# Both halves of the product of states and receptance on VectorE, with new order tables

## The reference, cut to what matters

```python
def step(s, rkvw):
    r_t, k_t, v_t, w_t = rkvw
    a = k_t[:, :, :, None] * v_t[:, :, None, :]
    out = jnp.einsum('bhk,bhkd->bhd', r_t, u * a + s)
    return (a + w_t[:, :, :, None] * s, out)
_, outs = jax.lax.scan(step, s0, xs)
att = jnp.moveaxis(outs, 0, 1).reshape(b, l, E)
```

## Time and profile before

| | before |
|---|---|
| three runs | 697.33, 699.70, 701.93 us, median 699.7 us |
| the profiled execution | 699.4 us, of which the span is 697.3 us |
| TensorE busy | 644.4 us (92%) |
| VectorE busy | 587.9 us (84%) |
| ScalarE busy | 575.3 us (83%) |
| GpSimd busy | 322.8 us (46%) |
| mean granted TensorE clock | 0.983 |

### The profile page before, as it was taken

The page is one execution under the profiler, slowest core; times in us unless marked ns, Lnnn a source line. Parts: engine busy times, 40 slices in busy tenths (PEclk is TensorE's granted clock), DMA queues, the critical chain, the costliest instruction groups (busy, mean ns, idle before and its releaser), DMA issues.

```text
span 697.3 us, 17053 instructions
## 1 busy us (share of the span) xinstructions
PE 644.4 (92%) x5763; PEld 559.7 (80%) x5763; DVE 587.9 (84%) x1420; ACT 575.3 (83%) x2083; POOL 322.8 (46%) x441
## 2 busy tenths in 40 slices
PE   6787999999999999999999999999999989797765
PEld 5566888898889898989889898889898868676654
DVE  2576579999999999999999999999999997858562
ACT  2689999899999999999999999999999986752311
POOL 1154362646455465636363746455465544324111
PEclk9999999999999999999999999999999999899999
DMA  8920032222323050505031222323040505050500
GB/s 302 325 70 9 1 86 53 75 64 62 85 55 92 15 131 2 144 2 136 11 104 43 76 70 62 85 56 90 16 130 2 144 2 136 2 132 6 136 8 8
DMA packets 54843, 52.77 MB, mean 76 GB/s; under 512 B 6126, under 2 KB 49510, under 8 KB 54374
## 3 DMA queue, kind: packets, MB, share of 16 engines
q1 hardware_dynamic: 54758, 51.70, 26.8%
HBM read 30.72 MB, written 4.19 MB: 50 GB/s over the span
## 4 chain that ended last, share of the span: by engine, by line
PE 74%; ACT 8%; DVE 8%; issue 4%; DMA 3%; POOL 2%; SPq 0%; POOLq 0%; DVEq 0%; ACTq 0%
PE PS_B L503 15%; PE PS_S L503 7%; PE PS_T L597 6%; PE PS_B L637 6%; PE PS_D L510 5%; PE PS_S L578 4%; PE PS_T L605 4%; PE PS_S L510 4%; PE PS_T L510 4%; ACT SC L1130 3%; PE PS_D L727 2%; PE PS_B L646 2%; DMA V<-values_by_head 2%; PE PS_B L659 2%; PE PS_D L503 2%
## 5 line engine op out<-in xcount | busy, mean ns | idle before, releaser
L1130 ACT ACTIVATE SC<-SC,NMX 128x128 f32<-128x128 f32 x512 | 200.6, 402 | 5.7 <-DVE NMX L876 5.4
L1130 ACT ACTIVATION_READ_ACCUMULATOR SC<-SC,NMX 128x1 f32 x512 | 103.1, 201 | 0.0
L876 DVE TENSOR_REDUCE NMX<-SC 128x4 f32<-128x512 f32 x128 | 84.5, 673 | 2.4 <-POOL SC L1299 1.7
L597 PE MATMUL PS_T<-CST,SC 128*128 128x128 f32 x512 | 78.7, 277 | 7.2 <-ACT PT L1138 3.0
L1138 ACT ACTIVATE PT<-PS_T 128x512 f32<-128x512 f32 x128 | 76.3, 596 | 9.6 <-PE PS_T L597 9.1
L597 PEld LDWEIGHTS PS_T<-CST,SC 128*128 128x128 f32 x512 | 60.1, 141 | 19.3 <-ACT SC L1130 7.8
L1341 POOL TENSOR_TENSOR SS<-SS,KR 128x1024 f32<-128x1024 f32 x16 | 37.8, 2363 | 76.8 <-DVE SS L948 76.8
L948 DVE TENSOR_TENSOR_SCAN SS<-W,AJ 128x1024 f32<-128x1024 f32 x32 | 73.1, 2284 | 0.0
L1299 POOL TENSOR_TENSOR SC<-SC,MADD 128x512 f32<-128x512 f32 x48 | 61.3, 1280 | 22.5 <-DVE SC L851 21.5
L1301 POOL TENSOR_TENSOR SC<-SC,MADD 128x512 f32<-128x512 f32 x32 | 40.7, 1272 | 59.9 <-DVE SC L851 59.9
L503 PE MATMUL PS_B<-MX,W 128*128 128x128 f32 x512 | 66.2, 278 | 0.8 <-ACT KR L1185 0.8
(11 more groups left out here) (161 smaller groups left out, 1589.5 us busy)
## 6 DMA issues: line engine op xcount, KB each, us to landing
W<-EW SPq DMA_DIRECT2D x32, 512.0 KB, 4.8
V<-values_by_head SPq DMA_DIRECT2D x32, 512.0 KB, 5.7
W<-in_weights SPq DMA_DIRECT2D x1, 4160.0 KB, 21.0
ENC<-in_enc SPq DMA_DIRECT2D x16, 128.0 KB, 2.4
values_by_head<-VC SPq DMA_DIRECT2D x16, 128.0 KB, 1.8
out<-X SPq DMA_DIRECT2D x16, 128.0 KB, 5.9
X<-in_x SPq DMA_DIRECT2D x1, 1920.0 KB, 15.9
W<-in_weights SPq DMA_DIRECT2D x1, 1280.0 KB, 8.6
```

What stands on the lines that cost most here:

```text
L597: last = pe.transpose(PS_T[:, j * T:(j + 1) * T], SC[:, nr(b, a) % 2, g, j, :], ident)
L876: dve.tensor_reduce(NMX[:, nr(b, a) % 2, GH * g:GH * g + GH], SC[:, nr(b, a) % 2, g], AX_X, ALU.max, negate=True)\
L1130: last = act.activation(SC[:, nr(b, a) % 2, g, j, :], SC[:, nr(b, a) % 2, g, j, :], ACT.Exp, bias=NMX[:, nr(b, a) % 2, h:h + 1], accum_out ...
```

## The change

`d_rstate` on VectorE takes the half as its argument and is listed twice in `DVE_ORDER`; GpSimd's `d_rstate` is gone. The product, its operands and the tile are the same. All five order tables are written anew.

```diff
-            def d_rstate(b, _):
-                dve.wait_ge(d_s, 2 * b + 1)
-                r = KR[:, 1, 0, :].unsqueeze(1).to_broadcast([P, RS, T])
-                dve.tensor_tensor(SS[:, 0], SS[:, 0], r, ALU.mult).then_inc(d_rs, 1)
+            def d_rstate(b, t):
+                dve.wait_ge(d_s, 2 * b + t + 1)
+                r = KR[:, 1, t, :].unsqueeze(1).to_broadcast([P, RS, T])
+                dve.tensor_tensor(SS[:, t], SS[:, t], r, ALU.mult).then_inc(d_rs, 1)
...
-            def d_rstate(b, _):
-                pool.wait_ge(d_s, 2 * b + 2)
-                r = KR[:, 1, 1, :].unsqueeze(1).to_broadcast([P, RS, T])
-                pool.tensor_tensor(SS[:, 1], SS[:, 1], r, ALU.mult).then_inc(d_rs, 1)
```

The tables of TensorE and VectorE. In VectorE's, the stretch with the scans is the end of the old table and the head of the new one:

```diff
 PE_ORDER = [
-    ("a_scores", 0, 1), ("a_prob_turn", (1, 1), 3), ("d_own", 0, 5), ("b_low2", 2, 4), ("a_prob_turn", (1, 2), 3),
-    ("d_read", 0, 5), ("b_decay1", 0, 4), ("a_prob_turn", (1, 3), 3), ("d_oturn", 0, 5), ("b_decay2", 0, 4),
...
-    ("a_out", 1, 3), ("a_key", 1, 2), ("b_valgate", 0, 4), ("b_valgate", 1, 4), ("d_yturn", 0, 5), ("a_query", 1, 2),
-    ("a_prob_turn", (0, 0), 1), ("a_scores", 1, 2), ("b_turn", 0, 3), ("d_out", 0, 5), ("a_prob_turn", (0, 1), 1),
-    ("a_turn", 0, 0), ("b_mlp1", 0, 3), ("b_mlp1", 1, 3), ("a_prob_turn", (0, 2), 1), ("b_mlp2", 0, 3),
-    ("d_turn", 0, 5), ("b_mlp2", 1, 3), ("a_val", 0, 0), ("a_prob_turn", (0, 3), 1), ("a_key", 0, 0), ("a_pv", 0, 1),
-    ("b_turn", 1, 3), ("d_keyrec", 0, 5), ("a_query", 0, 0), ("d_keyrec", 1, 5), ("a_out", 0, 1), ("b_low1", 0, 3),
-    ("d_val", 0, 5), ("a_prob_turn", (1, 0), 2), ("b_low2", 0, 3)]
+    ("d_val", 0, 6), ("a_prob_turn", (1, 1), 3), ("b_low2", 0, 4), ("a_scores", 0, 1), ("d_own", 0, 5),
+    ("a_prob_turn", (1, 2), 3), ("b_low2", 2, 4), ("d_read", 0, 5), ("b_decay1", 0, 4), ("a_prob_turn", (1, 3), 3),
...
+    ("a_prob_turn", (0, 0), 1), ("a_query", 1, 2), ("a_prob_turn", (0, 1), 1), ("d_yturn", 0, 5), ("a_scores", 1, 2),
+    ("a_prob_turn", (0, 2), 1), ("a_turn", 0, 0), ("d_out", 0, 5), ("b_turn", 0, 3), ("a_val", 0, 0),
+    ("b_mlp1", 0, 3), ("b_mlp1", 1, 3), ("b_mlp2", 0, 3), ("d_turn", 0, 5), ("a_prob_turn", (0, 3), 1),
+    ("b_mlp2", 1, 3), ("a_pv", 0, 1), ("d_keyrec", 0, 5), ("a_key", 0, 0), ("b_turn", 1, 3), ("a_out", 0, 1),
+    ("a_query", 0, 0), ("d_keyrec", 1, 5), ("a_prob_turn", (1, 0), 2), ("b_low1", 0, 3)]
 DVE_ORDER = [
-    ("d_own", 0, 5), ("b_streams", 1, 4), ("b_streams", 2, 4), ("a_mask", (0, 1), 1), ("a_inverse", 1, 3),
...
-    ("a_normal", 0, 0), ("d_sum", 0, 5), ("a_mask", (1, 1), 2), ("d_stats", 0, 5), ("d_moments", 0, 5),
-    ("a_maxima", (1, 0), 2), ("a_mask", (1, 2), 2), ("a_mask", (1, 3), 2), ("a_addmask", (1, 3), 2), ("d_ruk", 0, 4),
-    ("a_maxima", (1, 1), 2), ("a_maxima", (1, 2), 2), ("d_normal", 0, 5), ("d_outer", 0, 4), ("d_outer", 1, 4),
-    ("b_sum", 0, 3), ("b_stats", 1, 3), ("b_moments", 1, 3), ("d_mixed", 0, 5), ("a_inverse", 0, 1),
-    ("d_mixed", 1, 5), ("a_maxima", (1, 3), 2), ("b_normal", 1, 3), ("d_scan", 0, 4), ("a_context", 0, 1),
-    ("a_query", 0, 0), ("b_mixed", 0, 3), ("d_rstate", 0, 4), ("a_sum", 0, 1), ("d_scan", 1, 4), ("d_mixing", 0, 5),
-    ("a_stats", 1, 1), ("b_streams", 0, 3), ("a_mask", (0, 0), 0)]
+    ("a_inverse", 0, 2), ("a_maxima", (1, 2), 3), ("d_normal", 0, 6), ("d_outer", 0, 5), ("d_scan", 0, 5),
+    ("b_sum", 0, 4), ("b_stats", 1, 4), ("d_mixed", 0, 6), ("b_moments", 1, 4), ("d_mixed", 1, 6),
+    ("a_maxima", (1, 3), 3), ("a_context", 0, 2), ("b_normal", 1, 4), ("d_rstate", 0, 5), ("d_outer", 1, 5),
+    ("a_sum", 0, 2), ("a_query", 0, 1), ("b_mixed", 0, 4), ("d_scan", 1, 5), ("d_mixing", 0, 6), ("d_rstate", 1, 5),
+    ("b_streams", 0, 4), ("a_mask", (0, 0), 1), ("d_own", 0, 5), ("b_streams", 1, 4), ("a_mask", (0, 1), 1),
...
+    ("b_normal", 0, 3), ("a_mask", (1, 0), 2), ("d_gated", 0, 5), ("b_gate", 0, 4), ("a_mask", (1, 1), 2),
+    ("a_mask", (1, 2), 2), ("d_sum", 0, 5), ("a_maxima", (1, 0), 2), ("a_mask", (1, 3), 2), ("a_maxima", (1, 1), 2),
+    ("d_stats", 0, 5), ("d_ruk", 0, 4), ("d_moments", 0, 5), ("a_addmask", (1, 3), 2)]
```

More of the change, by code:

```diff
@@ L83 @@
 SP_ORDER = [
[L84 removed]
+    ("b_vspread", 0, 4), ("d_store", 0, 6), ("b_wspread", 0, 3), ("a_load", 0, 0), ("b_vstore", 0, 3)]
 PE_ORDER = [
[L86 to L88 removed]
@@ L112 @@
-ACT_ORDER = [
[L113 to L123, removed]
-    ("a_prob_copy", (0, 1), 1), ("b_gelu", 0, 3), ("a_scale", 0, 0), ("b_gelu", 1, 3), ("d_first_states", 0, 4),
-    ("a_exps", (0, 3, 1), 1), ("a_prob_copy", (0, 2), 1), ("d_scale", 0, 5)]
@@ L126 @@
-POOL_ORDER = [
-    ("b_addnorm", 0, 4), ("b_addnorm", 1, 4), ("a_addmask", (0, 0), 1), ("a_root", 1, 2), ("a_addmask", (0, 2), 1),
-    ("a_addbias", 0, 1), ("b_addnorm", 2, 4), ("a_addbias", 1, 2), ("d_final", 0, 6), ("b_root", 0, 3),
-    ("a_root", 0, 0), ("b_addbias", 0, 3), ("a_addmask", (1, 0), 2), ("a_addmask", (1, 1), 2),
-    ("a_addmask", (1, 2), 2), ("d_root", 0, 5), ("d_shift", 0, 5), ("b_root", 1, 3), ("b_shift", 0, 3),
-    ("d_rstate", 0, 4)]
+    ("d_val", 0, 6), ("a_prob_turn", (1, 1), 3), ("b_low2", 0, 4), ("a_scores", 0, 1), ("d_own", 0, 5),
@@ L133 @@
+POOL_ORDER = [
+    ("d_root", 0, 6), ("d_shift", 0, 6), ("b_root", 1, 4), ("b_shift", 0, 4), ("b_addnorm", 0, 4),
+    ("a_addmask", (0, 0), 1), ("b_addnorm", 1, 4), ("a_addbias", 1, 3), ("b_addnorm", 2, 4),
+    ("a_addmask", (0, 2), 1), ("d_final", 0, 6), ("a_addbias", 0, 1), ("a_root", 1, 2), ("a_root", 0, 0),
+    ("b_root", 0, 3), ("a_addmask", (1, 0), 2), ("b_addbias", 0, 3), ("a_addmask", (1, 1), 2),
+    ("a_addmask", (1, 2), 2)]
 LAG = max(lag for order in (SP_ORDER, PE_ORDER, DVE_ORDER, ACT_ORDER, POOL_ORDER) for _, _, lag in order)
@@ L1351, in _ @@
             pieces = named(a_root, b_shift, d_shift, d_final, a_addbias, a_addmask, b_root, b_addbias, b_addnorm,
-                           d_rstate, d_root)
+                           d_root)
             for i in range(B + LAG):
```

31 lines of the change are left out of this document (23 added, 8 removed).

## The result

The changed kernel takes 725.9 us (median of 4, 724.89 to 728.36), the kernel before in the same series 700.4 us (697.33 to 701.93): a ratio of 1.0375, 95% interval 1.0346 to 1.0403. I had forecast 700.3 us, at most 708. The page of the changed kernel begins as follows; the line of engines answers to the earlier trace rows.

What follows compares the result with a forecast made beforehand. TensorE was taken to bound the steady part, with VectorE close behind. Steady part -0.5 us and drain +1.3 us gave +0.8 us on the profiled 699.4, so 700.2; forecast against the median 700.3 us, range 694 to 708.

Steps and rivals of the forecast that it cites:

- What the product costs: Second product: 2.36 us on GpSimd, which nobody waits for in steady periods; 1.14 us more on VectorE, partly offset by removed gaps.
- the steady part: Repeating periods: 0.17 us gained and 0.1 to 0.2 lost per period, over some twelve periods; taken as -0.5 us.
- First stretch: From the MLP's second product to the decay: VectorE needs 13.45 us, TensorE 13.51, level; new waits of 0.1 to 0.2 us.
- The rival of a missed handoff: `b_sum` to `b_decay1` on VectorE runs 0.4 to 0.6 us longer and sets every period: 707.5 us, chance 0.18.
- Second stretch: Cross scores to the product: VectorE 10.2 to 10.6 us against TensorE's 10.43, level; `b_sum` up to 0.2 us late.
- The fill: Start of the run: no touched row changes by more than a few tenths; bounded by -1 and +1 us, taken as 0.
- My own sign of error: A fill shorter or longer by over 2 us before the first scan at about 114 us would show the forecast wrong.
- The drain: End of the run, where VectorE leads and additions to it show: three terms, +0.9, +0.9 and -0.5 us, sum +1.3 us.
- The wait of 3.21 us of the earlier trace: TensorE's wait for `b_normal 1` before 599.53, forecast to grow by 0.9 us with a scan ahead instead of an outer product.
- The last batch: No streams there; GpSimd's 2.36 us before the read become 1.22 plus 0.31 plus 0.4 us: -0.5 us.
- the locked GpSimd: VectorE locks GpSimd out at `b_shift`, making `b_mixed` 0.2 to 0.4 us late: 704 us, chance 0.08; no cost in the sum.
- lose its one listed wait: TensorE loses all its waits, 2.4 us over twelve periods and 1.3 us in the drain: 696 us, chance 0.14.

Runs made afterwards that it cites:

- the run without the product: Kernel before with its old tables, the second half of the states never multiplied on any engine: 697.2 us, ratio 0.9966.
- the tables alone: Changed kernel with all its new order tables, but the second product given back to GpSimd at the head of its table: 727.7 us, ratio 1.037.
- The run with the key and `b_normal` first: Changed kernel with `a_key 0` ahead of `a_pv 0` on TensorE and `b_normal 1` ahead of `a_context 0` on VectorE: 727.4 us, ratio 1.0384.

## Why the prediction was wrong

**What the product costs.** Right on GpSimd, where taking the work away gave nothing in the steady part: the earlier trace rows and the run without the product. Right on VectorE in the new order as well: 36.71 us of work and 0.6 us of gaps fit into 37.3. The new table has indeed removed gaps; in the old order, which keeps them, the same product costs 12 us.

**First stretch.** I gave VectorE 13.45 us from `b_sum` to the end of `b_streams 1`; in the trace after it takes 13.6 (315.33 to 328.93), and `b_decay1` starts 0.16 us behind its end. Its size was right, and so was "level". The rival of a missed handoff had this stretch as its place, and it isn't the place: no wait of TensorE for `b_streams` or `b_mixed` stands in the list above, and with the tables alone, where VectorE has 1.14 us less to do there, the period is the same.

**Second stretch: the step that failed.** VectorE's side was again right, 10.68 us (mask at 342.27, end of the scan at 352.95) against 10.2 to 10.6. TensorE's side was not. I took its 9.57 us from the old chain, added `a_val 0` and had 10.43; it takes 11.38 us (342.29 to the end of `b_mlp2 1` at 353.67), and then `a_pv` waits another 0.45. VectorE, which I had up to 0.2 us late at `b_sum`, is early there instead and waits 0.67 us for that product. I laid TensorE's pieces end to end and asked only whether VectorE would keep up with them; I never asked what TensorE would wait for in its own new order. For the steady part I forecast -0.5 us; it cost 12.7. In the chain after, TensorE's way from the scores to `a_pv` leaves the engine twice:

```profile
341.18 1.11 PE PS_S L578 x16
342.29 0.68 DVE SC L851
...
343.11 0.41 PE PS_S L496 x2
...
345.61 3.84 PE PS_B L503 x32
...
350.63 1.28 ACT L1130
...
353.58 0.49 ACT PT L1138
...
354.12 1.08 PE PS_T L605 x32
```

At 342.29 the turn behind the scores is held by the bank that the mask reads; the turn of probabilities ahead of it and the wait take 0.93 us from start to start instead of 0.44. At 349.44 the first MLP product ends, and ScalarE's way until 354.12, 4.68 us, holds a GELU, the load of a function table (1.28 us; its line in ScalarE's view is below), exponentials and two copies, where TensorE's own pieces fill 4.1 (the rest is the 0.45 of wait and short ones). In the old order `a_val 0` and `a_key 0` stood between the second MLP product and `a_pv`.

By the start-to-start distances of TensorE's instructions over seven periods, against before, the way through `b_mlp2` to `a_pv` is 0.71 us longer, that from `a_val 0` to the MLP 0.20, inside the MLP's first product 0.13, at `d_out` and at `d_yturn` 0.09 each: sum 1.2, from which small gains elsewhere go, for 1.03 us of period. (The turns of the probabilities, with the wait for the mask, are only 0.06 longer in sum, because the old wait of `a_scores` is gone.) The waits that the list shows grew from 0.17 to 0.72 us per period, about half of the loss. The other half stands in what the profile counts as busy. The groups of TensorE between 200 and 560 us, before first and then after:

```profile
L503 PE MATMUL PS_B<-B_LT,W 128*128 128x128 f32 x320 | 37.4, 275 | 0.0
...
L510 PE MATMUL PS_D<-W,YT 128*128 128x256 f32 x40 | 10.3, 380 | 0.0
L510 PE MATMUL PS_S<-W,A_LT 128*128 128x256 f32 x36 | 9.2, 379 | 0.0
```

```profile
L503 PE MATMUL PS_B<-B_LT,W 128*128 128x128 f32 x288 | 34.5, 278 | 0.0
...
L510 PE MATMUL PS_D<-W,YT 128*128 128x256 f32 x36 | 10.1, 403 | 0.0
L510 PE MATMUL PS_S<-W,A_LT 128*128 128x256 f32 x36 | 9.7, 391 | 0.0
```

The same products have got longer, 403 against 380 ns. It is only the first one behind a hand-over: of the four of `d_out` at 343.35 the first takes 0.47 us and the others 0.38, as all four do before. ScalarE's and then TensorE's lines show such hand-overs:

```profile
344.73 0.81 ACT L1077 ACTIVATE B_LT<-PS_B,COL 128x128 f32<-128x128 f32 x2 [0.37 <-PE PS_B L496]
348.10 1.14 ACT L1169 ACTIVATE HG<-PS_B,COL 128x128 f32<-128x128 f32 x4
...
350.63 1.28 ACT L1130 ACT_TABLE_LOAD   x1
```

```profile
345.59 3.84 PE L503 MATMUL PS_B<-B_LT,W 128*128 128x128 f32 x32
349.29 1.99 PE L637 MATMUL PS_B<-W,HG 128*128 128x256 f32 x8
```

`B_LT` is done at 345.54 and its product starts at 345.59; the first half of `HG` at 349.24, its product at 349.29. Before, the two products started 0.5 and 0.8 us after the end of what they read. So the new order has used up ScalarE's room ahead of TensorE, and waits short enough hide in TensorE's records.

That this makes the period is shown in so far as TensorE does the same work with the same product on GpSimd or on VectorE, and is longer by these waits. Which one of them rules is not shown: with one taken away, the period was 38.38 at best and up to 38.97, with other waits or with a chain over VectorE in its place, and each move changed the order at other places too. Whether some order holds 37.3 with the product on VectorE stays open.

**The fill.** I had bounded it by 1 us either way, since no row that the change touches was long there. It is the second failed step: 10.6 us to the first read. I had looked at the pieces that moved and priced their work, but in the fill engines wait for each other and the order itself is the cost. My own sign of error, a first scan that moves by over 2 us, came: 120.2 instead of 114.4. The two runs with exchanged first rounds show that rounds 0 to 2 hold much of the cause: 5 to 6 us that the old first rounds give back in the new order, 9 us that the new ones cost in the old. The first read of the former is still 5.5 us later than before, and where that comes from stays open. Which entry it is they don't show; moving `a_stats 1`, my suspect, gained nothing.

**The drain.** Forecast +1.3 us, measured +2.6, with other parts; that the sign came out is luck. The wait of 3.21 us of the earlier trace rows didn't grow but went: in all of the drain after 600 us `b_turn` waits 0.4 us for `b_normal`. The last batch gave -0.5 us from read to read, as I had it. The loss lies between the reads of batches 13 and 14, 36.0 us instead of 32.3. Of these 3.6 us some 1.5 are the clock: TensorE is busy for 28.59 us with the same 223 products at a granted clock of 0.95, and before for 27.12 at 1.00. The run with the key and `b_normal` first has the new tables and a clock of 1.00 there, and takes 34.4. The other 2.1 us are waits. TensorE's longest wait and then VectorE's there, after:

```profile
PE PS_D L503 <- DVE XK L1049: 2.6, 1, 2.6
```

```profile
DVE AJ L941 <- DMA V<-values_by_head: 4.2, 1, 4.2
```

`d_mixed` stands behind the first scan in the new table and behind a second outer product in the old one, and the first outer product ahead of either waits for the spread values, 4.2 us here and 2.9 before. TensorE's products of the channel mixing wait for both. The mechanism (a scan instead of an outer product ahead) was mine, at another piece, and I had not asked what VectorE itself waits for ahead of it. This part is read from the traces, not tested.

**The rivals and the locked GpSimd.** `b_shift` took 1.04 us (and 0.61 where nothing disturbed it, not the 0.70 that I read from another tile's row), and VectorE waited for it in no steady period: no cost, as in the sum. TensorE did lose its one listed wait, and got others. None of my rivals had an order that costs more than the work it moves.

## What to carry to other kernels

Where each engine runs a fixed order, a new order can cost more than the work that it moves, here all of it: run the new order without the moved work first, and the moved work in the old order. Before a forecast, follow for each engine that sets the pace what every piece waits for in the new order, over all engines, ScalarE too, and do it again for the first rounds; busy sums and two-engine stretches only say that the new order could work. Room on an engine is not its share without work: in the old order 1.35 us of 37.3 stood idle, and 0.4 us of that could be used.

## What was not expected of the hardware

A wait of about a tenth of a microsecond ahead of a product needn't show as a wait. The first product behind such a hand-over has a longer record, 0.47 instead of 0.38 us at `d_out`; the mean of that group went from 380 to 403 ns and of another from 379 to 391. TensorE's busy time in a period rose from 37.13 to 37.68 us with the same work. So its list of waits held only about half of the loss of 1.03 us, and the other half looked like work; the start-to-start distances had all of it and said where.
